# Expert rows summed in memory: each put adds to one of two rows per token and waits for the landing of the put before it

## The reference, cut to what matters

```python
E, K, H, F = 64, 6, 256, 96
CAP = 2 * (256 * K // E)          # 48 places per expert
topk_w, topk_ids = _grouped_topk(router_logits, bias)        # 6 experts per token
buf = zeros((E, CAP + 1, H)).at[se, slot].set(x[tok])[:, :CAP]   # tokens past the 48th of an expert are dropped
h = silu(einsum(buf, w_gate)) * einsum(buf, w_up)
out = einsum(h, w_down)
y = segment_sum(out[se, pos] * valid * w, tok, num_segments=Tn)  # each token sums its experts' rows
x = x + gb * (y + shared)
```

## Time and profile before

| | us |
|---|---|
| median of 3 runs | 386.42 (382.71 to 392.1) |
| profiled execution, its own time | 384.25 |
| profiled execution, span of the core | 382.5 |
| token stage and prologue | 0 to about 233 |
| pair stage, from the first get to the last put's issue | 234.2 to 338.2 |
| last stage, from SP's first load to the end of the span | 339.9 to 382.5 |

### The profile page before, as it was taken

One profiled execution on the slowest core, in us unless ns is written; L12 is line 12 of the kernel. 1 busy time (PEld: TensorE's weight loads), 2 busy tenths in 40 slices (PEclk: granted clock), 3 DMA queues, 4 the chain that ended last, 5 costly groups with the idle time before them and its releaser, 6 DMA issues.

```text
span 382.5 us, 7155 instructions
## 1 busy us (share of the span) xinstructions
PE 311.1 (81%) x2528; PEld 225.2 (59%) x2528; DVE 235.0 (61%) x927; ACT 136.3 (36%) x376; POOL 110.0 (29%) x146
## 2 busy tenths in 40 slices
PE   3699899989899898998988726859869989906865
PEld 2585777868788687886876513424424545504644
DVE  3856375788797977979677994232333345404777
ACT  4322314433557425574254570022222334500000
POOL 6220051130311312112122004756756554420000
PEclk9999998999999899998998665765955699965999
DMA  5960559696293881621410001458899721049994
GB/s 158 333 213 2 205 103 245 219 206 221 54 271 138 199 266 52 205 83 51 164 38 1 35 35 38 114 142 232 199 260 229 184 61 53 22 149 421 401 418 176
DMA packets 52724, 63.07 MB, mean 165 GB/s; under 512 B 4384, under 2 KB 48530, under 8 KB 52689
## 3 DMA queue, kind: packets, MB, share of 16 engines
q1 hardware_dynamic: 34224, 40.56, 35.9%
q10 hardware_dynamic: 15392, 15.47, 11.5%
q0 software_dynamic: 3072, 6.59, 6.8%
HBM read 43.27 MB, written 21.01 MB: 168 GB/s over the span
## 4 chain that ended last, share of the span: by engine, by line
PE 57%; DVE 18%; DMA 10%; issue 5%; ACT 4%; POOL 2%; SPq 1%; another core or an unknown queue 1%; POOLq 0%; DVEq 0%; ACTq 0%
PE ps_s L1488 9%; DVE scm L871 8%; DMA egu<-y_dram 7%; PE ps_s L1321 5%; PE ps_a L1239 4%; PE ps_b L1248 4%; PE ps_c L1272 4%; PE ps_s L1372 3%; PE ps_o L1342 3%; PE ps_c L1501 3%; PE ps_o L1501 3%; PE ps_s L1357 3%; PE ps_b L1477 3%; PE ps_s L1495 2%; PE ps_a L1260 2%
## 5 line engine op out<-in xcount | busy, mean ns | idle before, releaser
L871 DVE TENSOR_TENSOR scm<-ps_s,decay 128x2048 f32<-128x2048 f32 x16 | 36.7, 2292 | 23.3 <-PE ps_s L1321 23.3
L1488 PE MATMUL ps_s<-egu,x 128*64 128x192 f32 x256 | 36.3, 415 | 4.3 <-DVE x L1099 2.5
L1104 DVE SCALAR_TENSOR_TENSOR z<-z,ps_s 128x96 f32<-128x96 f32 x32 | 8.1, 254 | 35.9 <-issue 18.6
L563 ACT ACTIVATE h_both<-rise,place 128x128 bf16<-128x128 f32 x91 | 27.5, 401 | 4.4 <-DVE place L981 4.4
L1514 PE MATMUL ps_a<-egu,ident 128*128 128x256 f32 x48 | 14.0, 452 | 17.0 <-DVE egu L1126 17.0
L1488 PEld LDWEIGHTS ps_s<-egu,x 128*64 128x64 f32 x256 | 19.8, 168 | 13.3 <-issue 5.8
L659 ACT ACTIVATE z<-ps_s 128x96 f32<-128x96 f32 x32 | 8.0, 250 | 51.0 <-PE ps_s L1488 35.6
L427 POOL TENSOR_TENSOR fac<-fin,half_exp 128x2 f32<-128x2 f32 x8 | 5.5, 691 | 68.8 <-DVE fin L846 68.8
L438 POOL TENSOR_TENSOR w_gated<-w_proj,ga_row 128x512 f32<-128x512 f32 x8 | 10.2, 1275 | 52.5 <-PE ps_s L1321 32.7
L1126 DVE TENSOR_TENSOR egu<-egu 128x1536 f32<-128x1536 f32 x7 | 12.3, 1758 | 19.4 <-DMA egu<-y_dram 19.4
L1514 PEld LDWEIGHTS ps_a<-egu,ident 128*128 128x128 f32 x48 | 10.5, 225 | 20.3 <-issue 13.5
(11 more groups left out here) (258 smaller groups left out, 735.7 us busy)
## 6 DMA issues: line engine op xcount, KB each, us to landing
y_dram<-y_zeros ACTq DMA_DIRECT2D x8, 1536.0 KB, 6.3
egu<-y_dram SPq DMA_DIRECT2D x16, 768.0 KB, 11.6
egu<-in_L_ffn_w_gate SPq DMA_DIRECT2D x16, 384.0 KB, 7.1
egu<-in_L_ffn_w_up SPq DMA_DIRECT2D x16, 384.0 KB, 7.8
ed<-in_L_ffn_w_down SPq DMA_DIRECT2D x16, 384.0 KB, 8.7
h_dram<-h2row SPq DMA_DIRECT2D x8, 320.0 KB, 2.4
pre<-in_L_attn_x SPq DMA_DIRECT2D x8, 256.0 KB, 6.3
out<-pre ACTq DMA_DIRECT2D x7, 256.0 KB, 8.7
```

Source lines behind the costliest of these rows:

```text
L563: last = a.activation(ramp[:, n], rise[:], ACT.Relu, bias=place[:, n // TOPK, n % TOPK:n % TOPK + 1])
L871: v.tensor_tensor(scm[:].rearrange("p r j q t -> p (r j q t)"), ps_s[:].rearrange("p r n -> p (r n)"), decay[:].rearrange("p r j q t -> p ...
L1488: last = mm.matmul(e_gups[n][rows].rearrange("p (g f) -> p g f", f=F), xt[n][:, k, rows], egu[:, slot // 2, :, 2 * (slot % 2) + half, k], ...
```

## The change

`y_dram` shrinks from six rows per token to two, with 256 rows behind them for the empty places. A result of a pair's first expert goes to the token's row 0 and one of its second expert to row 1. The puts add to what stands in memory (`compute_op=ALU.add`), and since two puts can meet in the same row, each put first waits until its predecessor has landed. All puts count on one semaphore. Empty places get rows of their own behind the tokens' (twice the partition, plus one in the upper half), so all 112 rows of a put are written, where up to 96 were. The index tables come out of fewer operations. The zero fill shrinks to a third, with one more small fill ahead of the token steps. The last stage loads two rows per token, all eight batches have buffers of their own, the half sums on DVE go, and PE adds two rows per token, not three.

```diff
-YROWS = B * N * TOPK
+SUMS = 2
+YROWS = SUMS * (B * N + P)
-YBUF = 4
...
-            for n in range(OBUF // 2):
-                sp.wait_ge(S[f"st_put{n}"], 32 * ((PAIRS // 2 - 1 - n) // (OBUF // 2) + 1))
+            sp.wait_ge(S["st_put"], 16 * PAIRS)
...
-            for b in range(YBUF):
-                load_y(b)
-            for b in range(YBUF, B):
-                sp.wait_ge(S["y_sum"], b - YBUF + 1)
+            for b in range(B):
                 load_y(b)
...
             def put(q):
                 pool.wait_ge(S["ix_ready"], 2)
                 pool.wait_ge(S["e_evac"], q + 1)
+                seen(pool, S["st_put"], 16 * q)
                 g.indirect_dma_start(out=y_dram, out_offset=bass.IndirectOffsetOnAxis(ap=y_ix[0:USED, q:q + 1], axis=0),
-                                     in_=e_out[q % OBUF][0:USED], in_offset=None, bounds_check=last_y,
-                                     oob_is_err=False).then_inc(S[f"st_put{q % OBUF // 2}"], 16)
+                                     in_=e_out[q % OBUF][0:USED], in_offset=None, compute_op=ALU.add, bounds_check=last_y,
+                                     oob_is_err=True).then_inc(S["st_put"], 16)
...
-            pool.wait_ge(S["st_fill"], 16 * B)
+            pool.wait_ge(S["st_fill"], 16 * (B + 1))
...
-                    a.dma_start(fill_v[s], spread(y_zeros[:], 1, N * TOPK // P)).then_inc(S["st_fill"], 16)
+                    a.dma_start(fill_v[s], spread(y_zeros[:], 1, N * SUMS // P)).then_inc(S["st_fill"], 16)
...
+            a.dma_start(spill_v, spread(y_zeros[:], 1, SUMS)).then_inc(S["st_fill"], 16)
             token_steps(step, B - 1)
...
-                    seen(act, S[f"st_put{(q - 2) % OBUF // 2}"], 32 * ((q - 2) // OBUF))
+                    seen(act, S["st_put"], 16 * (q - 1 - OBUF))
...
-                v.tensor_scalar(pick_u[:], ps_a[:, PAIRS:2 * PAIRS], -1.0, float(P), ALU.mult,
+                v.tensor_scalar(tile_f[:], ps_a[:, PAIRS:2 * PAIRS], -float(P), float(B * N), ALU.mult,
                                 ALU.add).then_inc(S["prologue_step"], 1)
                 dve.wait_ge(S["prologue_step"], 9)
-                v.tensor_scalar(pick_t[:], pick_u[:], 248, None, ALU.bitwise_and).then_inc(S["prologue_step"], 1)
-                v.tensor_scalar(pick_j[:], pick_u[:], 7, None, ALU.bitwise_and).then_inc(S["prologue_step"], 1)
+                v.tensor_tensor(tok_ix[:], ps_a[:, 0:PAIRS], tile_f[:], ALU.add).then_inc(S["ix_ready"], 1)
+                v.tensor_tensor(tok_f[:], ps_a[:, 0:PAIRS], tile_f[:], ALU.add).then_inc(S["prologue_step"], 1)
...
-            def half_sums(b):
-
-                y = y_in[b % YBUF]
-                dve.wait_ge(S[f"ld_quad{b % YBUF}"], 96 + 16 * NT * (b // YBUF + 1))
-                v.tensor_tensor(y[:, :, 0:3], y[:, :, 0:3], y[:, :, 3:6], ALU.add).then_inc(S["y_half"], 1)
...
-                    for j in range(3):
-                        last = mm.matmul(ysum[b % 2][:, C * i:C * i + C], ident[:], y[:, i, j], start=(j == 0), stop=(j == 2))
+                    for j in range(2):
+                        last = mm.matmul(ysum[b % 2][:, C * i:C * i + C], ident[:], y[:, i, j], start=(j == 0), stop=(j == 1))
```

More of the change, by code:

```diff
@@ L181, in adaln_attention_moe @@
         picks = sb("picks", [P, 2 * PAIRS])
-        pick_u = sb("pick_u", [P, PAIRS], U32)
-        pick_t = sb("pick_t", [P, PAIRS], U32)
-        pick_j = sb("pick_j", [P, PAIRS], U32)
         tile_f = sb("tile_f", [P, PAIRS])
-        j_f = sb("j_f", [P, PAIRS])
+        spill = sb("spill", [P, PAIRS])
+        row4 = sb("row4", [P, 1])
+        upper_half = sb("upper_half", [P, 1])
         tok_f = sb("tok_f", [P, PAIRS])
@@ L224, in adaln_attention_moe @@
         abs_rows, sign_rows = sh_g[0:B], z2[0:B]
-        y_in = [flat[:, NT * TOPK * C * i:NT * TOPK * C * (i + 1)].rearrange("p (i j c) -> p i j c", i=NT, j=TOPK)
-                for i in range(YBUF)]
+        y_in = [flat[:, NT * SUMS * C * i:NT * SUMS * C * (i + 1)].rearrange("p (i j c) -> p i j c", i=NT, j=SUMS)
+                for i in range(B)]
         ygb = [z1, z2]
@@ L262, in adaln_attention_moe @@
         xt_taken wcol_ready gup ge_exp gh_ready htp ht_taken dnp e_evac
-        y_half y_sum y_gb y_out
-        """.split() + [f"ld_quad{i}" for i in range(QUADS)] + [f"ld_xr{i}" for i in range(XBUF)] + [f"st_put{i}" for i in range(OBUF // 2)] + [f"ld_x{b}" for b in range(3)]
+        y_sum y_gb y_out
+        """.split() + [f"ld_quad{i}" for i in range(QUADS)] + [f"ld_xr{i}" for i in range(XBUF)] + ["st_put"] + [f"ld_x{b}" for b in range(3)]
         S = {n: sem(n) for n in names}
@@ L274, in adaln_attention_moe @@
         h2_v = h2_dram[0:B * N].rearrange("(b i p) c -> b p i c", p=P, i=NT)
-        fill_v = y_dram.rearrange("(b p r) c -> b p (r c)", b=B, p=P).rearrange("b p (a n) -> b p a n", n=C)
-        y_v = y_dram.rearrange("(t p j) c -> t p (j c)", p=P, j=TOPK)
+        fill_v = y_dram[0:SUMS * B * N].rearrange("(b p r) c -> b p (r c)", b=B, p=P).rearrange("b p (a n) -> b p a n", n=C)
+        spill_v = y_dram[SUMS * B * N:YROWS].rearrange("(p r) c -> p (r c)", p=P).rearrange("p (a n) -> p a n", n=C)
+        y_v = y_dram[0:SUMS * B * N].rearrange("(t p j) c -> t p (j c)", p=P, j=SUMS)
         def token_steps(step, last):
@@ L355, in _ @@
                 load_quad(QUADS + k, k)
-            for n in range(OBUF // 2):
-                sp.wait_ge(S[f"st_put{n}"], 32 * ((PAIRS // 2 - 1 - n) // (OBUF // 2) + 1))
+            sp.wait_ge(S["st_put"], 16 * PAIRS)
             def load_y(b):
                 for i in range(NT):
-                    landed = S[f"ld_modb{i}"] if b == B - 1 else S[f"ld_quad{b % YBUF}"]
-                    sp.dma_start(y_in[b % YBUF][:, i].rearrange("p j c -> p (j c)"), y_v[NT * b + i]).then_inc(landed, 16)
-            for b in range(YBUF):
-                load_y(b)
-            for b in range(YBUF, B):
-                sp.wait_ge(S["y_sum"], b - YBUF + 1)
+                    landed = S[f"ld_modb{i}"] if b == B - 1 else S[f"ld_quad{b}"]
+                    sp.dma_start(y_in[b][:, i].rearrange("p j c -> p (j c)"), y_v[NT * b + i]).then_inc(landed, 16)
+            for b in range(B):
                 load_y(b)
@@ L410, in _ @@
             g.iota(row_ix[:], pattern=[[0, 1]], base=0, channel_multiplier=1, allow_small_or_imprecise_dtypes=True)
-            g.iota(pick_key[:].rearrange("p b (i j) -> p (b i) j", i=NT), pattern=[[-8, B * NT], [-1, TOPK]], base=P,
+            g.iota(pick_key[:].rearrange("p b (i j) -> p (b i) j", i=NT), pattern=[[-1, B * NT], [0, TOPK]], base=B * NT,
                    channel_multiplier=0, allow_small_or_imprecise_dtypes=True)
+            g.iota(row4[:], pattern=[[0, 1]], base=0, channel_multiplier=SUMS, allow_small_or_imprecise_dtypes=True)
             g.iota(row_base[:], pattern=[[-SLOTS, E]], base=ROWS + SHIFT, channel_multiplier=0,
@@ L1009, in indices @@
                 dve.wait_ge(S["unramped"], 1)
-                v.tensor_scalar(pick_u[:], ps_a[:, PAIRS:2 * PAIRS], -1.0, float(P), ALU.mult,
+                v.tensor_scalar(tile_f[:], ps_a[:, PAIRS:2 * PAIRS], -float(P), float(B * N), ALU.mult,
                                 ALU.add).then_inc(S["prologue_step"], 1)
                 dve.wait_ge(S["prologue_step"], 9)
-                v.tensor_scalar(pick_t[:], pick_u[:], 248, None, ALU.bitwise_and).then_inc(S["prologue_step"], 1)
-                v.tensor_scalar(pick_j[:], pick_u[:], 7, None, ALU.bitwise_and).then_inc(S["prologue_step"], 1)
+                v.tensor_tensor(tok_ix[:], ps_a[:, 0:PAIRS], tile_f[:], ALU.add).then_inc(S["ix_ready"], 1)
+                v.tensor_tensor(tok_f[:], ps_a[:, 0:PAIRS], tile_f[:], ALU.add).then_inc(S["prologue_step"], 1)
                 dve.wait_ge(S["prologue_step"], 10)
-                v.tensor_scalar(tile_f[:], pick_t[:], P / 8.0, None, ALU.mult).then_inc(S["prologue_step"], 1)
+                v.tensor_scalar(upper_half[:], row_ix[:], float(SLOTS), None, ALU.is_ge)
+                v.tensor_scalar(spill[:], tok_f[:], float(B * N), row4[:, 0:1], ALU.is_ge, ALU.mult).then_inc(S["prologue_step"], 1)
+                dve.wait_ge(S["prologue_step"], 11)
+                v.tensor_scalar(spill[:], spill[:], upper_half[:, 0:1], None, ALU.add).then_inc(S["prologue_step"], 1)
                 dve.wait_ge(S["prologue_step"], 12)
[L1018 to L1023, removed]
+                v.scalar_tensor_tensor(out=y_ix[:], in0=tok_f[:], scalar=float(SUMS), in1=spill[:], op0=ALU.mult,
                                        op1=ALU.add).then_inc(S["ix_ready"], 1)
@@ L1119, in _ @@
             pair_steps(pair_step)
-            def half_sums(b):
-                y = y_in[b % YBUF]
-                dve.wait_ge(S[f"ld_quad{b % YBUF}"], 96 + 16 * NT * (b // YBUF + 1))
-                v.tensor_tensor(y[:, :, 0:3], y[:, :, 0:3], y[:, :, 3:6], ALU.add).then_inc(S["y_half"], 1)
[L1128 to L1133, removed]
-            for b in range(B - 1):
[L1136 to L1140, removed]
```

(7 more changed lines are left out.)

4 lines of the change are left out of this document (2 added, 2 removed).

## The result

The changed kernel takes 435.37 us (median of 4 runs, 432.47 to 436.7) where the kernel before took 386.58 us (median of 4) beside it: a ratio of 1.129, with a 95% interval of 1.1175 to 1.1404. Medians here are of all runs of a job; ratios and intervals use only its fast runs, those within 1.5% of the fastest of the same kernel. The profiled execution has a span of 432.4 us.

A forecast was written before the change was run, and what follows sets the result against it. The chain of puts, each waiting for its predecessor, was taken as the bound: 255.0 + 32 × 4.15 − 0.8, plus 6 contention, gives 393.0; plus last stage 24.6 is 417.6. Execution 419.4, against the median 421.5 us (390 to 460).

The forecast's parts named there:

- The first put: Start of the pair stage's first put: at 255.0 us, 0.6 earlier than before through the shorter index tables.
- The period without the weights: Pair stage, one put's start to the next: 2.53 landing + 0.80 to next start + 0.82 adding = 4.15 us.
- The contention: Pair stage while later experts' weights load: some 12 puts take 0.5 us more each, 6 us.
- The landing: End of the pair stage: last put lands 0.80 us less than a period after its start, at 393.0 with contention.
- The last stage: From the last put's landing to the end: 24.6 us, 18.0 less than before, paced by PE's 64 products.
- the one in which adding is hidden: Rival, pair stage: adding is hidden in the put, period 3.3 to 3.5 us, 389 us, no change; chance 0.20.
- The fast one: Rival, pair stage: POOL sees the landing during the get, no 0.80 us, period 2.6 us, 379 us; chance 0.06.
- The long period: Rival, pair stage: adding costs its own transfer or longer POOL issue, period 4.7 to 6.7 us; chance 0.20.
- PE would stay at the lower level in the last stage: Rival, last stage: PE's 64 products take 29 us in place of 17.8, adding 11 us; no separate chance.
- the fills: Zero fills, ahead of and within the token stage: smaller fills' saving and the added fill both priced at nothing.

## Why the prediction was right, point by point

The forecast was 421.5 us (390 to 460) and slower with a chance of 0.80. Its cause held. Its sum came out 14 us short, and the terms differ by more than that:

- **The first put.** Forecast for 255.0, it started at 253.3: 1.7 us less.
- **The period without the weights.** Forecast at 4.15 us, measured 4.41 over 25 periods, with single ones at 4.3. Start to landing is 3.5 to 3.6 us (forecast 2.53 + 0.82 = 3.35) and from the landing to the next start 0.77 to 0.82 (forecast 0.80). For what adding costs, the difference between a get and a put (0.82) came near in size (measured 1.0), but by luck in part, since it is another cost: half of the extra time is spent on POOL. The 4.41 includes two periods of 5.3 and 4.75 us between 322 and 333, which stay unexplained. Over 31 periods it makes 8 us more.
- **The contention.** This is the term that was mis-sized. I had 6 us (0.5 for each of 12 puts), from the share of busy DMA time and no row. Measured are six periods of 7.1 us, not twelve with 0.5 each: 16 us more than six of 4.41. Between the first put and the last, taking the loads out gave back 17 us (across two jobs), and spacing them 15 (within one). The error was to price it as packets that share engines in turn. As I read it, a put waits for a good part of what is queued, and a group of four experts puts 1.2 MB into the queues at once. How the DMA engines share their time between the two, packet by packet, no run here shows.
- **The landing** came 0.2 us later than forecast for the last put.
- **The last stage.** Forecast at 24.6 us, measured 22.6. PE's first product came 3.6 us after SP's first load, as forecast, but only the first eight products were at the lower level (3.42 us), not twelve. PE had idled 56 us before them (forecast: some 40).

The sum of these is −1.7 + 8.1 + 16.2 − 6 + 0.2 − 2.0 = +14.8 us, the difference between the forecast span (417.6) and the measured one (432.4).

Of the rivals, the one in which adding is hidden fell with the 1.0 us that the plain puts showed. The fast one fell with the 0.77 to 0.82 us from landing to start in every period. The long period (4.7 to 6.7) was right for the first six periods and more, though its reason was not: plain puts have such periods too, and without the loads adding ones have none. That PE would stay at the lower level in the last stage did not happen. What I had taken at nothing, the fills, can't be told from nothing: the first get comes at 232.0 and 230.3 us in the two profiles of the changed kernel, and at 230.7 to 241.1 in the seven with the old fills.

By the Trainium skill's fixed 2.0 us and 436 GB/s (DMA: Bandwidth & Descriptors, Anatomy of one DMA) a put would take 2.3 us (an estimate); the plain ones took 2.5 to 2.6 when nothing was queued, and 7.8 to 8.1 beside the weights, which no term of that formula has. The prediction took these 2.3 us for a whole period; with the 0.8 us to the next start it would be 3.1.

One thing was missed that did not decide. I took the kernel before as a fixed 386 us. It has executions near 361 too, and the changed kernel, which hangs on landings and not on PE's clock, was at 435 in both jobs in which it ran. Both of these jobs had the kernel before near 387, so against 361 (a ratio near 1.2) it was not measured.

## What to carry to other kernels

Before ordering transfers one behind the other, multiply: number of transfers by (start to landing + 0.8 us to the next start), and compare it with the pace of what feeds them. Here 32 times 4.4 us stood against a pace of 2.6, and a saving of 20 us could not pay for it. Take the landing time from rows in which the queues are as full as they will be: behind a burst of loads it was 1.6 to 3.1 times that of the idle case. If a chain is needed all the same, space the loads that run beside it, and keep several chains.

## What the runs showed of the hardware

- An adding indirect DMA of 112 rows of 1 KB occupies POOL for 1.45 us against 0.95 for a plain one, and lands 3.5 to 3.6 us after its start against 2.5 to 2.6.
- Off the chain, adding cost nothing that could be measured beside a kernel before near 387 us (ratio 0.994). POOL then needs 3.1 us for a put and a get back to back, against 2.58 with plain puts, and can set the pace.
- A put beside bursts of weight loads landed after 5.6 to 8.4 us (a plain one after 7.8 to 8.1); with one load of 384 KB outstanding it took about 3.6.
- The same kernel, unchanged, took 360.33 and 397.39 us in two executions, with PE's granted clock mostly at the higher or the lower level in the pair stage (28 of the 37 us).
